# Handing part of the score maxima of the first self attention to ScalarE

## The reference

```
h = layernorm(x)
q, k, v = h Wq, h Wk, h Wv                 # per head 16 channels, fake-quantised weights
P = softmax(q k^T * 16^-0.5)               # 1024 x 1024 per head
x = (P v) Wo + bo + x
```

## Time and profile before

| | us |
|---|---|
| median of three runs | 4137.87 |
| lowest and highest of them | 4121.34, 4141.66 |
| the profiled execution | 4131.29 |
| its span | 4128.5 |
| the sixteen steps of the first self attention, from the first shifted scores | 211.0 to about 933 |

### The profile page before, as it was taken

The page is one execution under the profiler, slowest core; times in us unless marked ns, Lnnn a source line. Parts: engine busy times, 40 slices in busy tenths (PEclk is TensorE's granted clock), DMA queues, the critical chain, the costliest instruction groups (busy, mean ns, idle before and its releaser), DMA issues. The chain is left out here.

```text
span 4128.5 us, 63035 instructions
## 1 busy us (share of the span) xinstructions
PE 3835.3 (93%) x23695; PEld 2391.4 (58%) x23695; DVE 2710.5 (66%) x4469; ACT 2378.3 (58%) x3310; POOL 1860.5 (45%) x1220
## 2 busy tenths in 40 slices
PE   3799999995998998998999999999999969999899
PEld 2544443433557886885555555555555537777787
DVE  6599999953536754435666676666766547665665
ACT  2477777772443334445777777777777744443332
POOL 1287891001202102005788877878878743222200
PEclk9799999997779999999999999999999989999999
DMA  5745344405622006883222222222222110000100
GB/s 167 179 63 73 61 53 53 44 2 99 106 39 57 19 13 214 313 318 135 82 79 86 77 82 93 78 83 90 80 82 73 47 41 10 3 9 1 43 16 16
DMA packets 314174, 328.16 MB, mean 79 GB/s; under 512 B 129592, under 2 KB 232952, under 8 KB 309520
## 3 DMA queue, kind: packets, MB, share of 16 engines
q1 hardware_dynamic: 311216, 315.17, 28.5%
q0 software_dynamic: 2656, 8.97, 0.8%
HBM read 195.47 MB, written 127.55 MB: 78 GB/s over the span
## 5 line engine op out<-in xcount | busy, mean ns | idle before, releaser
L1840 POOL TENSOR_TENSOR f_sums<-f_sums,f_probs 128x1024 f32<-128x1024 f32 x384 | 917.0, 2388 | 116.8 <-ACT f_probs L1985 78.3
L1859 DVE TENSOR_REDUCE f_mx<-f_s 128x1 f32<-128x512 f32 x992 | 634.9, 682 | 338.7 <-PE f_s L2010 330.9
L1985 ACT ACTIVATE f_probs<-f_st 128x1024 f32<-128x1024 f32 x512 | 520.4, 1016 | 327.9 <-PE f_st L2054 327.7
L1528 ACT ACTIVATE f_probs<-f_st 128x512 f32<-128x512 f32 x1024 | 535.9, 601 | 168.6 <-PE f_st L1586 168.3
L1397 DVE TENSOR_REDUCE f_mx<-f_s 128x1 f32<-128x512 f32 x960 | 599.9, 682 | 29.2 <-PE f_s L1548 6.8
L1953 ACT ACTIVATE f_st<-f_shift 128x1024 f32<-128x1024 f32 x512 | 526.6, 1029 | 23.0 <-DMA f_shift<-shift 6.9
L2070 PE MATMUL f_acc<-f_probs,f_v 128*64 128x512 f32 x2048 | 496.2, 606 | 0.0
L2010 PE MATMUL f_s<-f_k,f_q 64*128 64x512 f32 x2976 | 479.3, 412 | 4.7 <-DVE f_mx L1859 4.7
L2010 PEld LDWEIGHTS f_s<-f_k,f_q 64*128 64x128 f32 x2976 | 268.3, 184 | 245.3 <-DVE f_mx L1859 127.9
L2054 PE MATMUL f_st<-f_q,f_k 64*128 64x512 f32 x3072 | 399.2, 390 | 5.2 <-ACT f_st L1953 5.2
L1586 PE MATMUL f_st<-f_q,f_k 50*128 50x512 f32 x1024 | 333.3, 474 | 6.9 <-ACT f_probs L1528 6.8
(11 more groups left out here) (377 smaller groups left out, 7839.9 us busy)
## 6 DMA issues: line engine op xcount, KB each, us to landing
q<-f_stage SPq DMA_DIRECT2D x80, 512.0 KB, 2.8
k<-f_stage SPq DMA_DIRECT2D x80, 512.0 KB, 2.8
f_q<-q SPq DMA_DIRECT2D x32, 1024.0 KB, 5.0
f_k<-k SPq DMA_DIRECT2D x32, 1024.0 KB, 7.3
f_shift<-shift SPq DMA_DIRECT2D x32, 1024.0 KB, 4.7
v<-f_v_stage SPq DMA_DIRECT2D x64, 256.0 KB, 2.9
f_v<-v SPq DMA_DIRECT2D x32, 512.0 KB, 3.9
f_q<-q SPq DMA_DIRECT2D x96, 128.0 KB, 4.4
```

What stands on the lines that cost most here:

```text
L1528: a_.activation(probs[:, n % NP, e % 2, :], stb[k % 3][:, :], ACT.Exp, scale=L.scale).then_inc(p_ready, 1)
L1840: g_.tensor_tensor(out, out, probs[:, n % NP, :, :], ALU.add).then_inc(sum_done, 1)
L1859: v.tensor_reduce(mx[:, i % 2, c:c + 1], bank[u % 3][:, :], AX_X, ALU.max).then_inc(s_free, 1)
L1985: a_.activation(probs[:, s % NP, :, :], stb[s % 2][:, :, :], ACT.Exp, scale=L.scale).then_inc(p_ready, 1)
```

## The change

In each slot of the plain scores whose number is odd (`joined`), for steps 1 to 15, the r = 0 head is handled otherwise. For its first half (f = 0) PE makes two matmuls into the bank, one with the first 512 keys and one, ahead of it, with the negated second 512 keys (`minus`), so that the bank holds the first half's scores minus the second half's. ScalarE takes the Relu of it into SBUF (`aside`). The second half (f = 1) is made as before. VectorE skips the first half's tile, and for the second half adds `aside` and takes the maximum in one instruction (`tensor_tensor_reduce`, with its full-size result to `larger`). Since max(a, b) = b + relu(a - b), this is the maximum over both halves. The r = 1 head is handled as before.

The Relu stands in ScalarE's list ahead of the third exponential of the slot (and ahead of `o_hi`). The bank of the first half's tile is now freed by ScalarE, through a semaphore `copied` of its own, and VectorE's count `s_free` skips it; all waits on `s_free` are put in terms of `vector_to(u)`. ScalarE also makes one negated copy of half of the keys for each step (`negate_keys`, 48 rows), at s = 13 ahead of the first exponential.

```
+        def joined(slot):
+            return slot % 2 == 1
...
+        taken = [at[u] for u in order if u[0] == "s" and joined(u[2]) and u[3:] == (0, 0)]
+        joins = [at[u] for u in order if u[0] == "s" and joined(u[2]) and u[3:] == (1, 0)]
+        place = {u: n for n, u in enumerate(taken)}
+
+        def copied_to(u):
+            return sum(1 for x in taken if x <= u)
+
+        def vector_to(u):
+            return u + 1 - copied_to(u)
...
                     for r in range(2):
                         u = at["s", i, slot, f, r]
+                        if u in place:
+                            continue
                         dve.wait_ge(s_ready, u + 1)
                         c = ((r * 2 + j) * QB + qb) * 2 + f
+                        if joined(slot) and r == 0:
+                            n = place[at["s", i, slot, 0, 0]]
+                            dve.wait_ge(copied, n + 1)
+                            v.tensor_tensor_reduce(larger[:, :], bank[u % 4][:, :], aside[:, n % 2, :], 1.0, -3.0e38, ALU.add, ALU.max,
+                                                   mx[:, i % 2, c - 1:c]).then_inc(s_free, 1)
+                            continue
                         v.tensor_reduce(mx[:, i % 2, c:c + 1], bank[u % 4][:, :], AX_X, ALU.max).then_inc(s_free, 1)
...
+                def set_aside(i, slot):
+                    u = at["s", i, slot, 0, 0]
+                    n = place[u]
+                    act.wait_ge(s_ready, u + 1)
+                    if n >= 2:
+                        act.wait_ge(s_free, vector_to(joins[n - 2]))
+                    a_.activation(aside[:, n % 2, :], bank[u % 4][:, :], ACT.Relu).then_inc(copied, 1)
+
+                def negate_keys(i):
+                    cur = i % DEPTH
+                    act.wait_ge(q_in[cur], (i // DEPTH + 1) * QLOADS)
+                    if i > 2:
+                        act.wait_ge(s_ready, at["s", i - 2, SLOTS - 1, 0, 0] + 1)
+                    a_.activation(minus[0:SROWS, i % 2, :], k_[cur][0:SROWS, 1, HALF:N], ACT.Copy, scale=-1.0).then_inc(minus_done, 1)
+
+                negate_keys(1)
+                for slot in range(EARLY):
+                    if joined(slot):
+                        set_aside(1, slot)
...
                     for s in range(SLOTS if i < STEPS else 10):
+                        n, slot = (i + 1, EARLY + s) if s < SLOTS - EARLY else (i + 2, s - SLOTS + EARLY)
+                        held = (n, slot) if n < STEPS and joined(slot) else None
                         for e in range(4):
+                            if e == 0 and s == 13 and i + 2 < STEPS:
+                                negate_keys(i + 2)
+                            if e == 2 and held:
+                                set_aside(*held)
...
+                def bank_free(u):
+                    pe.wait_ge(s_free, vector_to(u - 4))
+                    if copied_to(u - 4):
+                        pe.wait_ge(copied, copied_to(u - 4))
+
...
-                        pe.wait_ge(s_free, u - 3)
+                        bank_free(u)
+                        gap_here = u in place
+                        if gap_here:
+                            pe.wait_ge(minus_done, i)
+                            t.matmul(bank[u % 4][:, :], q[cur][rows, j, qb * P:(qb + 1) * P], minus[rows, i % 2, :],
+                                     start=True, stop=False, tile_position=(64 * r, 0))
                         t.matmul(bank[u % 4][:, :], q[cur][rows, j, qb * P:(qb + 1) * P], k_[cur][rows, j, f * HALF:(f + 1) * HALF],
-                                 start=True, stop=True, tile_position=(64 * r, 0)).then_inc(s_ready, 1)
+                                 start=not gap_here, stop=True, tile_position=(64 * r, 0)).then_inc(s_ready, 1)
```

More of the change, by code:

```diff
@@ L1293, in attend_narrow @@
             slots_of, two = range(DEPTH), range(2)
+            aside = sb("aside", [P, 2, 512])
+            larger = sb("larger", [P, 512])
+            copied, minus_done = sem("copied"), sem("minus_done")
+            minus = sb("minus", [64, 2, HALF], F32R)
             q = [sb(f"q{k}", [P, 2, N], F32R) for k in slots_of]
@@ L1343, in maxima @@
                     slot = i % DEPTH
-                    sp.wait_ge(s_free, at["turn", i] + 1)
+                    sp.wait_ge(s_free, vector_to(at["turn", i]))
                     for r in range(2):
@@ L1410, in negate @@
                     else:
-                        dve.wait_ge(s_free, at["s", i, SLOTS - 1, 1, 1] + 1)
+                        dve.wait_ge(s_free, vector_to(at["s", i, SLOTS - 1, 1, 1]))
                     v.tensor_reduce(negm[:, :], mx[:, i % 2, :].rearrange("p (c f) -> p c f", f=2), AX_X, ALU.max,
@@ L1455, in project @@
                                         ALU.add).then_inc(s_free, 1)
-                v.memset(mx[:, 0, :].rearrange("p (c f) -> p c f", f=2)[:, :, 1:2], -3.0e38).then_inc(mx_set, 1)
+                v.memset(mx[:, :, :].rearrange("p s (c f) -> p (s c) f", f=2)[:, :, 1:2], -3.0e38).then_inc(mx_set, 1)
                 for slot in range(SLOTS):
@@ L1611, in rows @@
                     half, u = n % 2, at["rows", n // 2, n % 2]
-                    pe.wait_ge(s_free, at["back", n // 2, half] + 1)
-                    pe.wait_ge(s_free, u - 3)
+                    pe.wait_ge(s_free, vector_to(at["back", n // 2, half]))
+                    bank_free(u)
                     for k in range(4):
@@ L1618, in project @@
                 def project(i, half):
-                    pe.wait_ge(s_free, at["rows", i, half] + 1)
+                    pe.wait_ge(s_free, vector_to(at["rows", i, half]))
                     pe.wait_ge(w_low, 1)
```

## The result

The changed kernel takes 4169.5 us, the median of seven runs (4158.66 to 4182.57), the kernel before 4137.87, likewise of seven (4121.34 to 4144.79). The medians lie 31.6 us apart; the ratio of the runs is 1.0093 (95% interval 1.0073 to 1.0113, which is 30 to 47 us), so the changed kernel is slower. Forecast was 4165 in a range of 4136 to 4190. Its profiled execution took 4168.64 us with a span of 4166.8.

What follows compares the result with a forecast made beforehand. Ordinary slots were taken as bound by a 2.61 us chain through ScalarE's first exponential, not VectorE. Terms 21.2 + 9.0 + 1.4 - 1.0 + 0.7 = +31.3 us on 4131.3 made 4162.6, given as 4165, range 4136 to 4190.

Steps and rivals of the forecast that it cites:

- Main step, the banks: Slots with a fifth unit (back, rows): fourth score's load waits for the Relu to free its bank; 0.73 and 0.64 us each.
- VectorE's relief is worth nothing in ordinary slots: Joined slots: 0.60 us less VectorE work gains 0, as VectorE already idles 0.21 of each 2.61 us slot.
- The rival with VectorE as pace: VectorE's maxima set the slot through the fourth score's bank wait; 120 joined slots save 0.60 each, -72 us, 4059; 8%.
- The rival by which the fourth score's 0.16 is given back: 176 ordinary slots each lose that wait for VectorE, -28 us, while fifth-unit waits come as forecast: 4134; 9%.
- ScalarE's part at nothing: Added Relu (0.58 us) per joined slot and negated key copy per step fit ScalarE's free time; cost 0.
- PE's part at nothing in ordinary slots: Extra 48-row score matmul per joined slot, 0.23 us, hides in PE's 0.30 us of waiting, 0.07 to spare.
- the rival of the added matmul: The extra score matmul isn't hidden: 0.23 us in each of 74 ordinary joined slots, +17 us, 4182; 9%.
- ordinary slots still 2.61 us, joined or not: Expected sign in the trace: slots without a fifth unit keep their length; below 2.60 would make the forecast wrong.
- the slot's last maximum at +2.77: VectorE's final maximum in joined slot 12 (i even) starts 2.77 us after slot start, where it was 2.58.
- The turn at even i: Slot s = 13, waiting for the negated maxima: 0.2 us later, 7 times, +1.4 us; odd i -0.14 each, -1.0.
- The join at 0.69: VectorE's adding maximum (tensor_tensor_reduce) taken as one pass of 0.69 us, followed at 0.61; ends 0.68 and 1.37.
- the rival of two passes: The adding maximum takes 1.37 us, delaying the next slot's scores: 0.5 us x 120, +60 more, 4225; 6%.

Runs made afterwards that it cites:

- e1: Changed kernel, joining only odd slots without a fifth unit (77 of 120): ratio 1.0018 to the kernel before; steps 1 to 14 +5.67 us.
- e2: Changed kernel, joining only odd slots that have a fifth unit: ratio 1.0093 to the kernel before; steps 1 to 14 +31.13 us.
- e7: Changed kernel, PE waiting before each unit only for the semaphore of the engine freeing its bank, not both: ratio 1.0147 to the kernel before.
- e4: Kernel before, one maximum per odd slot over 64 keys instead of 512, exponentials' scale a millionth (result differs): ratio 0.9989; steps 1 to 14 -4.41 us.
- e8: Kernel before, one more 64-column maximum on VectorE ahead of each slot's last maximum: ratio 1.0019; steps 1 to 14 +2.38 us.
- e11: Kernel before, each slot's first exponential over half its columns, scale a millionth (result differs): ratio 0.9918; steps 1 to 14 -23.15 us.
- e5: Kernel before, plus an SBUF-to-SBUF Relu on ScalarE that nobody waits for, at 119 of 120 places: ratio 1.0031; steps 1 to 14 +0.35 us.
- e3: Changed kernel, Relu ahead of the second exponential instead of the third: ratio 1.0060 to the kernel before; steps 1 to 14 +15.77 us.
- e6: Kernel before, first score matmul of each odd slot's r = 0 head issued twice: ratio 1.0049; steps 1 to 14 +11.00 us.
- e12: Changed kernel, joining only slots without a fifth unit and Relu ahead of the second exponential: ratio 1.0013 to the kernel before; steps 1 to 14 +0.52 us.

## Why the prediction was right

Main step, the banks: right in place, cause and nearly in size. e1 and e2 put 31.1 of 36.9 us into slots with a fifth unit. The term was 0.73 and 0.64 per slot and measured 0.80 and 0.70: about 0.06 of each is the second semaphore in front of the load (e7), which the forecast's 0.05 from end to load did not hold. The Relu's 0.62 was nearly the 0.60 that this working used, though the forecast had named 0.58.

How near the total came is in part luck. For steps 1 to 14 the forecast's terms make 30.6 us and 36.9 were measured; that the medians lie 31.6 apart, next to the forecast's 31.3, owes to the rest of the program, which scatters by more than that gap (last section). By the ratio of the runs it is 38.

That VectorE's relief is worth nothing in ordinary slots: right, by e4 and e8 from either side, and e11 shows the chain that sets them. The rival with VectorE as pace falls (it wanted -54 in e4, measured -4.4). By "Perfetto Trace Analysis" (the Trainium skill, Engine Utilization) a well-optimised kernel has at least one engine near full use; here VectorE is at 93% and has no part in the pace of an ordinary slot, so that nearness says nothing of what its relief is worth. The rival by which the fourth score's 0.16 is given back falls by e4 too.

ScalarE's part at nothing: right (e5). By "ScalarE: Activation LUTs" (the Trainium skill, Rules for kernel authors) relu is VectorE's work and not ScalarE's; the work itself costs 0.35 us in 14 steps here. What costs is the Relu's place in ScalarE's order, behind two exponentials (e3).

PE's part at nothing in ordinary slots: right (e6, 2.61), and the rival of the added matmul falls with it. In the others it was put at 0.1 to 0.2 and taken to go under in the Relu's wait; alone it is 0.23 there (e6), and under the longer wait it does not show.

Wrong in size: "ordinary slots still 2.61 us, joined or not". The slot behind an ordinary joined one is 0.05 longer, 3.0 us in all. The forecast placed the slot's last maximum at +2.77; it comes at +2.87. The adding maximum starts 0.13 after the Relu's end where 0.05 was taken (it too has two waits, one of which is an EVENT_SEMAPHORE of its own in the trace; that this is the difference was not tried), and the next maximum follows it at 0.62 where 0.61 was taken. e3 takes the late maximum away and the 0.05 with it. The turn at even i costs 0.30 and not 0.2, and e3 has it at 3.17, so the late maximum is its cause too; at odd i it gains 0.20 and not 0.14. The join at 0.69 was right, and the rival of two passes (1.37) falls: the read of its accumulator, 0.08, runs beside the next maximum.

## What to carry to other kernels

Before relieving the engine with the largest share, write one period down as a chain of starts and waits; what closes it is the pace, and an engine busy 93%, as VectorE here, can have no part in it. When the release of a buffer moves to another engine, ask where in that engine's own order the releasing instruction stands, and which slots need the buffer again within the same period: there the new engine's whole queue stands in the path.

## What the runs showed of the hardware that was not expected

The granted clock of TensorE in step 15, where no scores run ahead and PE has fewer matmuls (198 in 42 us, against 3904 in 634), differs between executions, and moves the whole program by up to 15 us. Three tables by stretches of that step, of the kernel before, the changed kernel and e3 (the clock is the number after POOL and its count; the second row of e3 is a part of one slot's length):

```profile
890.60:933.00 42.40, 36.99 (x198) 11.76 (x195) 2.05 (x5) 32.77 (x63) 0.00 (x0) 0.92 0.00 1
```

```profile
925.80:966.00 40.20, 34.53 (x199) 11.17 (x195) 2.06 (x5) 32.87 (x64) 0.00 (x0) 1.00 0.00 1
```

```profile
907.40:962.10 54.70, 50.42 (x196) 14.27 (x192) 2.05 (x5) 33.05 (x64) 0.00 (x0) 0.63 0.00 0
915.00:919.00 4.00, 4.00 (x20) 1.49 (x16) 0.68 (x2) 2.77 (x5) 0.00 (x0) 0.50 0.00 0
```

To the start of its last slot the step takes 39.5 us at 1.00, 42.2 at 0.92 and 54.7 at 0.63; where it is 0.50, the lower level (1.2 GHz), an ordinary slot takes 4.07 in place of 2.61. The step has the same instructions in the kernel before, the changed one, e1 to e8 and e12: five of these eleven profiled executions took 39.5, three 42.2, and e2, e7 and e3 took 47.1, 50.7 and 54.7. What follows the step, also the same in all eleven, took between 3191 and 3206 us. So where a few us count, the same steps at full clock are the better measure than the median of the whole. Whether a kernel's timing ahead of step 15 makes the fall likelier was not tried.
